# A T5 pair phase with its output projection a step later, a choice phase that fetches expert weights ahead of the row scatter, and weight loads moved to an earlier phase

## The reference, cut to what matters

```
for i in range(4):
    nx = t5_layer_norm(h, ln1[i])
    q, k, v = nx @ attn_q[i], nx @ attn_k[i], nx @ attn_v[i]      # 12 heads of 64
    attn = softmax(einsum('bqhd,bkhd->bhqk', q, k) + bias)         # 16 tokens each
    h = h + (attn @ v) @ attn_o[i]
    nx = t5_layer_norm(h, ln2[i])
    y = relu(nx @ ffn_wi[i]) @ ffn_wo[i]
    if i in (1, 3):
        y = y + moe_ffn(nx, gate_w[mi], moe_w1[mi], moe_w2[mi])    # top 2 of 8 experts, gelu
    h = h + y
return t5_layer_norm(h, ln_f)
```

## Time and profile before

| | before |
|---|---|
| runs | 1822.48, 1823.77, 1829.81 us; median 1823.77 |
| profiled execution | 1819.51 us, of which the profile's span is 1817.7 |
| PE busy | 1431.2 us (79%), mean granted clock 0.837 |
| DVE, ACT, POOL busy | 648.7, 467.2, 460.4 us |
| pair phase, first turn of the loop | from 303.35 us (first turn of unit 0) to 577.1 |
| choice phase, first turn | 578.36 to 632.2 us |
| pair and choice phase, second turn | from 765.64 and from 1035.79 us |

### The profile page before, as it was taken

How to read it: one execution, slowest core, us unless ns; L and a number is a source line. 1 busy time by engine, 2 the same in 40 slices (tenths; PEclk the granted TensorE clock), 3 DMA queues, 4 the chain that set the end, 5 groups by cost and what they waited for, 6 DMA issues and landing times. The chain is left out here.

```text
span 1817.7 us, 35567 instructions
## 1 busy us (share of the span) xinstructions
PE 1431.2 (79%) x14426; PEld 1136.1 (62%) x14426; DVE 648.7 (36%) x1668; ACT 467.2 (26%) x1226; POOL 460.4 (25%) x597
## 2 busy tenths in 40 slices
PE   5469743999987699589998769948735995876998
PEld 5255422788775489478877549934525995453766
DVE  3444652333232122233333222244551223463334
ACT  0420331333332011133333211113201332321121
POOL 0000461222221434222222143412324442230000
PEclk8778856999877899799998788979557998856999
DMA  4010006000000464400000047413015453010000
GB/s 119 0 27 12 5 1 228 2 2 2 2 2 2 166 214 125 122 18 2 2 3 2 1 160 234 133 53 111 3 75 184 146 173 116 8 55 4 27 27 17
DMA packets 57392, 117.44 MB, mean 65 GB/s; under 512 B 16656, under 2 KB 43540, under 8 KB 52400
## 3 DMA queue, kind: packets, MB, share of 16 engines
q1 hardware_dynamic: 40144, 60.38, 11.1%
q0 software_dynamic: 17088, 54.81, 8.6%
HBM read 140.33 MB, written 24.87 MB: 91 GB/s over the span
## 5 line engine op out<-in xcount | busy, mean ns | idle before, releaser
L1774 PE MATMUL bank<-t_wo,t_ctx 128*128 128x192 f32 x384 | 95.7, 416 | 29.0 <-ACT t_xa L1785 27.0
L1774 PEld LDWEIGHTS bank<-t_wo,t_ctx 128*128 128x128 f32 x384 | 86.6, 251 | 30.4 <-ACT t_ctx L1835 30.1
L1296 PE MATMUL bank<-xT,w 96*128 96x512 f32 x192 | 86.8, 611 | 15.5 <-ACTq L1350 15.5
L1149 PE MATMUL bank<-t_ew,t_hg 128*128 128x192 f32 x552 | 97.2, 327 | 0.0
L1389 DVE SCALAR_TENSOR_TENSOR h<-bank,cw,h 128x192 f32<-128x192 f32 x128 | 53.5, 418 | 100.3 <-PE bank L1312 83.8
L1149 PEld LDWEIGHTS bank<-t_ew,t_hg 128*128 128x128 f32 x552 | 88.7, 190 | 0.2
L329 PE MATMUL bank<-ident,rows 128*96 128x128 f32 x112 | 25.2, 418 | 77.1 <-DVE rows L312 77.1
L1181 ACT ACTIVATE t_hg<-bank 128x384 f32<-128x384 f32 x92 | 40.1, 488 | 173.2 <-PE bank L1137 140.3
L1177 ACT ACTIVATE l_hg<-bank,l_ew 128x128 f32<-128x128 f32 x186 | 51.4, 375 | 121.1 <-PE bank L1137 89.5
L1035 POOL DMA_INDIRECT t_ew<-in_t_moe,source x46 | 46.7, 1014 | 138.7 <-DVE t_og L1217 132.1
L1133 PE MATMUL bank<-t_xgT,t_ew 128*128 128x128 f32 x552 | 74.8, 289 | 4.2 <-DVE t_xgT L1208 3.3
(11 more groups left out here) (329 smaller groups left out, 3052.8 us busy)
## 6 DMA issues: line engine op xcount, KB each, us to landing
rows_in<-blank SPq DMA_DIRECT2D x2, 2967.0 KB
t_xg<-rows_in SPq DMA_DIRECT2D x46, 129.0 KB
wA<-in_t_wqkv SPq DMA_DIRECT2D x9, 576.0 KB
t_wo<-in_t_wo SPq DMA_DIRECT2D x9, 576.0 KB
t_qkv<-in_t_wqkv SPq DMA_DIRECT2D x9, 576.0 KB
w<-in_l_w SPq DMA_DIRECT2D x8, 576.0 KB, 5.3
rows_in<-blank SPq DMA_DIRECT2D x1, 3999.0 KB
l_xg<-rows_in SPq DMA_DIRECT2D x31, 129.0 KB
```

The source lines that it names most:

```text
L1149: mm = pe.matmul(k.bank[6 + b % 2][:, 0:DIM], k.hg[b % 2][:, m, :], w[:, SPLIT + m * DIM:SPLIT + (m + 1) * DIM], start=(m == 0), stop=(m = ...
L1296: mm = pe.matmul(k.bank[(u * FC + m) % 4][:], k.w1[s][:, c, m * P:(m + 1) * P], k.xT[:, c, n * HALF:(n + 1) * HALF], start=(c == 0), stop= ...
L1774: mm = pe.matmul(turn_bank[:, 0:DIM], buf.ctx[a % 2][:, m, :], layer(a).wo[:, m, :], start=(m == 0), stop=(m == FC - 1))
```

## The change

- Pair phase. On PE the output projection of w = s - 2 stands between queries and keys of step s (it was that of s - 1 at the step's end). The turn of n stands right after the keys, the turn of w after the values. ACT's list is reordered to match; its copy of the context stands ahead of the exponential for w >= 8 and at the end of the step else. DVE and POOL make the first norm's root and rows two units ahead instead of one.
- Choice phase. PE counts behind one pair of the hidden blocks instead of three. `plan_blocks` makes `source` first and `place_i` after it; POOL fetches the four weights, then scatters the rows.
- Loads. The tensors of a turn's first layer are allocated earlier, and their first contents are loaded in `quant_projection_phase` instead of the T5 norm phase. Those of the second layer (now in `wA`) are loaded in the pair phase, where PE waits for them at unit 8. `expert_blocks_phase` loads 8 tensors instead of 13.

```diff
     link(dve.tensor_reduce(first, square, AX_X, ALU.add))
-    dve.wait_ge(k.counted, 2)
...
-    dve.tensor_copy(k.place_i[:], k.place[:]).then_inc(k.chosen, 1)
     link(dve.tensor_tensor(end, first, used, ALU.add))
...
     dve.tensor_tensor(k.source[:, 0:nb], source, k.same[:, 0:nb], ALU.add).then_inc(k.chosen, 1)
+    dve.wait_ge(k.counted, 2)
...
+    dve.tensor_copy(k.place_i[:], k.place[:]).then_inc(k.chosen, 1)
...
@@ -1691,22 +1691,31 @@
                 return pe.transpose(turn_bank[:, P:2 * P], k.rows[:, u % NT, P:C_TOKEN], k.ident[:])
 
             for s in range(-1, units + 2):
-                u, a, w = s, s - 1, s - 2
+                u, a, w, n = s, s - 1, s - 2, s + 1
                 if 0 <= u < units:
                     qkv, x = layer(u).qkv, buf.xa[u % 2]
+                    if u == NT:
+                        pe.wait_ge(k.loaded, 16 * len(loads))
                     pe.wait_ge(k.first_kept, u + 1)
-                    if w >= 1 and w - 1 < NT:
-                        pe.wait_ge(k.relu_a, w)
-                        pe.wait_ge(k.relu_v, w)
                     features(pairs[0], qkv[:, 0, :], x).then_inc(k.q_made, 1)
-                    if u >= 2:
-                        pe.wait_ge(k.ctx_copied, u - 1)
+                if 0 <= w < units:
+                    pe.wait_ge(k.ctx_copied, w + 1)
+                    for m in range(FC):
+                        mm = pe.matmul(turn_bank[:, 0:DIM], buf.ctx[w % 2][:, m, :], layer(w).wo[:, m, :],
+                                       start=(m == 0), stop=(m == FC - 1))
+                    mm.then_inc(k.projected, 1)
+                if 0 <= u < units:
                     features(pairs[1], qkv[:, 1, :], x).then_inc(k.k_made, 1)
-                if 0 <= w < units:
-                    pe.wait_ge(k.normed_second, w + 1)
-                    pe.wait_ge(k.doubled_second, w + 1)
-                    turn(w).then_inc(k.turned_second, 1)
+                if n < units:
+                    pe.wait_ge(k.normed_first, n + 1)
+                    pe.wait_ge(k.doubled_first, n + 1)
+                    if w >= 0:
+                        pe.wait_ge(k.added, w + 1)
+                    turn(n).then_inc(k.turned_first, 1)
...
+                    if u == 1:
+                        pe.wait_ge(k.v_kept_a, 1)
+                        pe.wait_ge(k.v_kept_v, 1)
...
+                if 0 <= w < units:
+                    pe.wait_ge(k.normed_second, w + 1)
+                    pe.wait_ge(k.doubled_second, w + 1)
+                    if n < units:
+                        pe.wait_ge(k.first_kept, n + 1)
+                    turn(w).then_inc(k.turned_second, 1)
...
-                if 0 <= a < units:
-                    pe.wait_ge(k.ctx_copied, a + 1)
-                    pe.wait_ge(k.first_kept, min(s + 2, units))
...
+            def keep_context(a):
+                act.wait_ge(k.pv_done, a + 1)
+                if a >= 2:
+                    act.wait_ge(k.projected, a - 1)
...
+                if w >= NT and a < units:
+                    keep_context(a)
...
+                if w < NT and a >= 0:
+                    keep_context(a)
...
-            norm(0, 0, k.scaled_first, k.normed_first)
+            for u in range(2):
+                norm(u, 0, k.scaled_first, k.normed_first)
...
-                if s + 1 < units:
-                    norm(s + 1, 0, k.scaled_first, k.normed_first)
+                if s + 2 < units:
+                    norm(s + 2, 0, k.scaled_first, k.normed_first)
...
-            double(0, 0, k.squared_first, k.scaled_first, k.doubled_first)
-            pool.wait_ge(k.doubled_first, 1)
+            for u in range(2):
+                double(u, 0, k.squared_first, k.scaled_first, k.doubled_first)
+            pool.wait_ge(k.doubled_first, 2)
...
-                if s + 1 < units:
-                    double(s + 1, 0, k.squared_first, k.scaled_first, k.doubled_first)
+                if s + 2 < units:
+                    double(s + 2, 0, k.squared_first, k.scaled_first, k.doubled_first)
...
             pool.wait_ge(k.chosen, 2)
+            for i in range(W_SLOTS):
+                fetch_expert(pool, k, i, nb, weights)
+            pool.wait_ge(k.chosen, 3)
             send_rows(pool, k)
             pool.sem_inc(k.owner_known, 1)
-            pool.wait_ge(k.chosen, 3)
-            for i in range(W_SLOTS):
-                fetch_expert(pool, k, i, nb, weights)
...
-            first(0)
+            first(0, 0)
             pe.wait_ge(k.chosen, 1)
...
-            first(1)
-            pe.wait_ge(k.chosen, 2)
+            for i in range(2, 2 * FC, 2):
+                first(i // FC, i % FC)
+            pe.wait_ge(k.chosen, 3)
             second(0)
             second(1)
...
+        early = stage()
+        one = Kern()
+        one.qkv, one.wi = tensor(early, "t5_qkv", [P, 3, SPLIT]), tensor(early, "t5_wi", [P, SPLIT])
+        one.wo, one.wo2 = (tensor(early, f"t5_{name}0", [P, FC, DIM]) for name in ("wo", "wo2"))
+        one.ln1, one.ln2 = (tensor(early, f"t5_{name}0", [P, 2]) for name in ("ln1", "ln2"))
+
+        def pair_loads(first):
+
+            return ([(one.qkv[:, i, :], a["t5_wqkv"][first, :, i, :]) for i in range(3)]
+                    + [(one.wo[:], a["t5_wo"][first]), (one.wi[:], a["t5_wi"][first]), (one.wo2[:], a["t5_wo2"][first]),
+                       (one.ln1[:], a["t5_ln1"][first]), (one.ln2[:], a["t5_ln2s"][first])])
...
-            quant_projection_phase(k, k.wA[0:CH, 0:2 * 3 * DIM].rearrange("p (c n) -> p c n", c=2), qi, ki, qx, vx)
+            quant_projection_phase(k, k.wA[0:CH, 0:2 * 3 * DIM].rearrange("p (c n) -> p c n", c=2), qi, ki, qx, vx,
+                                   loads=pair_loads(0))
...
-            one.qkv = k.wA[:, 0:3 * SPLIT].rearrange("p (w n) -> p w n", w=3)
-            two.qkv = tensor(st, "t5_qkv", [P, 3, SPLIT])
...
-            norm_phase(k, k.h, 1e-5, loads=pair_loads(0) + [(bias16[:], a["t5_bias16"]), (k.bias[:], a["t5_lnf"])])
+            two = Kern()
+            two.qkv, two.wi, two.wo2 = k.wA[:, 0:3 * SPLIT].rearrange("p (w n) -> p w n", w=3), k.w1s[0][:, 0:SPLIT], k.w2[0]
+            two.wo, two.ln1, two.ln2 = tensor(st, "t5_wo1", [P, FC, DIM]), tensor(st, "t5_ln11", [P, 2]), k.ln2s
+
+            norm_phase(k, k.h, 1e-5, loads=[(bias16[:], a["t5_bias16"]), (k.bias[:], a["t5_lnf"])])
...
-                                  loads=[(two.wi, a["t5_wi"][2 * r + 1]), (two.wo2[:], a["t5_wo2"][2 * r + 1]),
+                                  loads=[(two.qkv[:], a["t5_wqkv"][2 * r + 1]), (two.wo[:], a["t5_wo"][2 * r + 1]),
+                                         (two.ln1[:], a["t5_ln1"][2 * r + 1]), (two.wi, a["t5_wi"][2 * r + 1]), (two.wo2[:], a["t5_wo2"][2 * r + 1]),
...
-    layers = (0, 1, 2, 3, 3, 3)
+    layers = (0, 1, 2, 3, 3)
```

More of the change, by code:

```diff
@@ L1028, in plan_blocks @@
     dve.tensor_tensor(k.source[:, 0:nb], source, k.same[:, 0:nb], ALU.add).then_inc(k.chosen, 1)
+    dve.wait_ge(k.counted, 2)
+    base = k.base[:, :, 0:n_e]
+    link(dve.scalar_tensor_tensor(base, first.unsqueeze(1).broadcast_to([P, NT, n_e]), float(P),
+                                  rank_bank[:, 0:NT * n_e].rearrange("p (t e) -> p t e", e=n_e), ALU.mult, ALU.add))
+    for c in range(2):
+        link(dve.tensor_tensor(k.picked[:, c, :, 0:n_e], k.sel[:, c, :, 0:n_e], base, ALU.mult))
+        link(dve.tensor_reduce(k.place[:, c, :], k.picked[:, c, :, 0:n_e], AX_X, ALU.add))
+    link(dve.tensor_tensor(k.picked[:, 0, :, 0:n_e], k.sel[:, 1, :, 0:n_e],
+                           k.iota[:, 0:n_e].unsqueeze(1).broadcast_to([P, NT, n_e]), ALU.mult))
+    link(dve.tensor_reduce(k.rows[:, :, C_SECOND], k.picked[:, 0, :, 0:n_e], AX_X, ALU.add))
+    dve.tensor_copy(k.place_i[:], k.place[:]).then_inc(k.chosen, 1)
 def fetch_expert(pool, k, i, nb, weights):
@@ L1791, in _ @@
             keep_turned(buf.xa[0], layer(0).ln1).then_inc(k.first_kept, 1)
+            def keep_context(a):
+                act.wait_ge(k.pv_done, a + 1)
+                if a >= 2:
+                    act.wait_ge(k.projected, a - 1)
+                banks = pairs[1] + pairs[2]
+                for j in range(QUADS):
+                    ins = act.activation(buf.ctx[a % 2][:, :, j * QUAD:(j + 1) * QUAD],
+                                         banks[j][:, 0:FC * QUAD].rearrange("p (m q) -> p m q", q=QUAD), ACT.Copy)
+                ins.then_inc(k.ctx_copied, 1)
             for s in range(units + 2):
@@ L1800, in _ @@
                     ins.then_inc(k.q_kept, 1)
+                if 0 <= w < units:
+                    act.wait_ge(k.added, w + 1)
+                    square(w, 1).then_inc(k.squared_second, 1)
+                if u < units:
                     act.wait_ge(k.k_made, u + 1)
@@ L1818, in _ @@
                     act.activation(buf.v[u % 2][:, 0:FF // 2], pairs[2][0][:, 0:FF // 2], ACT.Copy).then_inc(k.v_kept_a, 1)
+                if 0 <= w < units:
+                    act.wait_ge(k.turned_second, w + 1)
```

(11 more changed lines are left out.)

107 lines of the change are left out of this document (25 added, 82 removed).

## The result

| | runs | median |
|---|---|---|
| before | 1821.43, 1822.48, 1823.77, 1829.81 us | 1823.12 |
| after | 1732.31, 1735.08, 1737.48, 1737.93 us | 1736.28 |

The ratio is 0.951, with a 95% interval of 0.949 to 0.953: 87 us less. The profiled execution of after took 1732.31 us, its span is 1730.4 and its mean granted clock 0.860.

What follows compares the result with a forecast made beforehand. PE was taken to bound the T5 pair phase, never idle in plain steps but waiting 2.31 us in gate steps. Gains 54.1 + 11.0 + 18.4 = 83.5 us; 1823.8 - 83.5 = 1740 us, range 1725 to 1762.

Steps and rivals of the forecast that it cites:

- Plain steps: Pair phase, plain steps: PE's work stays 15.70 us and a new wait of 0.3 makes the step 16.0 us.
- new wait of 0.3: Plain step, PE before wi, waiting for the second norm's turned rows copied by ACT: 0.3 us, bounds 0 and 0.63.
- Gate steps: Pair phase, gate steps: 11.8 us of PE work plus a 0.6 us wait before PV, 12.4 us instead of 17.1.
- Ends: Pair phase, first queries to projection 14: 223.8 us against 253.3 and 248.4 before, gains 29.5 + 24.6 = 54.1 us.
- Loads: T5 norm phase without its 13 loads: bias phase starts 11.0 us earlier, bounds 9.6 and 12.3; block phase gains nothing.
- Choice phase: Choice phase with early counts and fetches before scatters: 9.2 us less per loop turn, 18.4 in all, bounds 4 and 13.
- The queue: Choice phase, POOL's queue: scattered rows stand behind the weights, early scatters land late, the last does not; sum unchanged.
- Rival 3: Choice phase: POOL cannot write scatter descriptors while weights are on their way; gain 4 per turn, time 1751; chance 0.07.
- rival 2: Pair phase: the new waits are not there, time 1728, or 1721 with `second` not drawn out either; chance 0.10.

Runs made afterwards that it cites:

- late_values: The changed kernel with three 128x768 memsets on DVE ahead of its copy of the values in steps 11 to 15; median 1764.45 us.
- before_again: The kernel before, unchanged, run once more for its profile beside the second group of variants; 1820.46 us (one run).
- after_again: The changed kernel, unchanged, run once more beside its variants in the second group; median 1728.51 us.
- both_first: The changed kernel with DVE's values copy ahead of its norm and, in plain steps, ACT's turned rows for w ahead of its values copy; median 1719.92 us.

## Why the prediction was right, point by point

- **Plain steps.** 16.0 predicted, 15.89 measured, but not for my reason. ACT's `keep_turned` stands where I laid it, and its copy of the values starts 2.35 us behind PE's values as in the earlier trace rows, but the two overlap and the rows are ready at 353.45, as PE comes at 353.50. The 0.19 above before's 15.70 is in PE's own segments: projection 347.51 - 345.46 = 2.05 (1.95 before), `wo2` 359.06 - 357.00 = 2.06 (1.96), the turn ahead of the scores 0.1 longer, the keys 0.1 shorter, the rest even. So the step of the prediction that failed is the new wait of 0.3; its bound of 0 was the right end, and the 0.19 that stood in its place was in no term, so that 16.0 fits by luck.
- **Gate steps.** 12.4 predicted; 12.59 measured with the wait, 12.5 on the average of a loop turn's. The wait before PV is 0.36 and not 0.6 and is missing in the last two, the gate 0.64 and not 0.5, turns and projection a little longer. That the wait of 2.31 took the clock with it, and that a short one would not, carried most of the term. Before has one gate step with the same wait at the full clock, from PV (L1740) to PV in the second loop turn:

```profile
930.30 1.16 PE L1740 MATMUL bank<-t_ptb,t_v 32*64 32x32 f32 x96
...
944.64 1.08 PE L1740 MATMUL bank<-t_ptb,t_v 32*64 32x32 f32 x86
```

It took 14.35 us; the steps with the same wait and a projection of 4.18 us took 17.0 to 17.1. So of the 4.5 us that a step lost, about 2.75 are clock and 1.75 the shorter wait and what else changed. late_values confirms that a wait put in brings the clock down, with costs of 1.5 to 3.1 us.
- **Ends.** 223.8 us from the first queries to projection 14 predicted (6 x 12.4 is 74.4 and not 74.6, so 223.6), 222.85 measured. Behind it I had left everything as before; at the full clock projection 14 itself took 2.22 instead of 4.21, and from its start to the choice phase 1.3 us were gained. Pair phases in all: 54.1 predicted, 31.8 + 27.3 = 59.1 in the first profiles, 28.8 + 25.8 = 54.6 between before_again and after_again. One after_again phase contains a stretch at a lower clock, behind 0.94 us in which PE issued nothing.
- **Loads.** 11.0 predicted, 17.10 - 6.05 = 11.05 measured from DVE's scaled rows to the bias phase; every profile with the loads moved has 6.0 to 6.1 there, every one without 16.7 to 17.2. That the quantised projection phase hides them holds (26.57 us before, 26.44 after). That fewer loads give the block phases nothing holds too: they were 2.7 and 1.6 us shorter in the first profiles, but between before_again and after_again 2.2 longer and 1.3 shorter.
- **Choice phase.** The mis-sized term: 9.2 per loop turn predicted; 7.2 and 7.5 with the hole, 11.8 and 12.4 without. Two steps failed. The fetches start 10.1 us behind the start of the phase and not 8.4: counts at 5.2 instead of 4.4, since the first hidden blocks run at a granted clock of 0.56 (0.67 before), and 4.9 from counts to fetch instead of 4.1, of which 0.97 stand between DVE's last operation and POOL's first issue (0.31 ahead of the first scatter before). And I let `second` be drawn out for good. Without the hole it ends 36 to 37 us behind the start, the x rows end last, and the next phase starts at 41.2 to 42.3, near the other bound I gave, 13.
- **The queue.** Rival 3 is out: 20 indirect transfers in a row, the scatters 1.28 to 1.33 us apart and the fetches 1.3 to 1.6, with no stop, so the stop that I derived from the Trainium skill ("DMA: Bandwidth & Descriptors", section "SWDGE vs HWDGE vs iDMA") does not occur at this depth. Its other rule, in the section "Two DMAs through the same engine are not ordered" (within one queue of an engine, descriptors start in order), agrees with the trace: in the first loop turn of after_again the scatters' packets (4128 bytes) start at 562.9, though the first scatter was issued at 554.0, and by then all but 10 of the weights' 512 (9216 bytes) have started. Its early scatters land 9.8 us behind their issue, its last 2.5, before_again's all about 2.5. As worked out in the prediction, that costs nothing, since the last scatter comes when the weights are through.

Scatters of after_again (553 to 556 and 570 to 576 us) and before_again (592 to 596): issues, median us to landing.

```profile
rows_in<-rows,place_i POOLq DMA_INDIRECT x2, 9.8
```

```profile
rows_in<-rows,place_i POOLq DMA_INDIRECT x4, 2.5
```

```profile
rows_in<-rows,place_i POOLq DMA_INDIRECT x3, 2.5
```

The total, 1740, was within 4 us of the first median, 1736.28, and part of that is luck: the pair phases gained 5 us more than their term, the block phases 4.3 that no term had, and the choice phases 3.7 less, held back by the hole. Where the hole is absent the forecast is 10 to 12 us too high (1728.51, 1729.89): inside the range of 1725 to 1762, but below the forecast's own 1731 to 1752 and at the 1728 that rival 2 gave for both waits missing.

## What to carry to other kernels

When PE waits a few us for a turned or copied tile in every step, it can pay to move the consumer a step later instead of speeding the producer: here the wait of 2.31 us took 2.75 us of clock with it in most steps. An order written out by hand is worth a layout of every engine's list against PE's, since the place of the wait that comes next is then known: of the two waits laid out here one was 0.36 us and not 0.6, the other did not come. Where one engine issues all indirect transfers, putting those with the long landing first was worth 6.7 us per phase here; splitting them left a long one to end alone and cost 2.7 to 2.9.

## What the runs showed of the hardware that I had not expected

- A hole in the instructions of two engines at once: in the first profile of after, PE issued five matmuls in 6.7 us and DVE left finished banks for 10.95 us, and PE came back 2 us behind the end of the last scatter (570.91 against 568.96); before's first profile has one too. The same programs did not show it in their later profiles. The cause is open.
- A small one is in every profile but late_values': within PV of the second gate step of each loop turn PE issues nothing for 0.3 to 1.2 us, whatever the kernel (before 0.41, after 0.29, after_again 0.94, both_first 1.07 in the first turn).
- A wait of 3.0 us on PE was followed by 3.8 us at a granted clock of 0.59 in one loop turn and by 4.7 us at 0.50 in the other. In before, a wait of 2.31 us was followed by a projection of 4.18 us in seven steps and of 2.19 in one, so the same wait does not always cost the clock.
- The same twelve matmuls of 128x192 take 2.05 us from start to the next group's start where the group ahead of them uses 64 or 32 of PE's rows (queries or PV, in after), and 1.95 where it uses 128 (turns or `wo2`, in before). The keys show the same: 2.41 us behind the queries' last group in before, 2.30 behind the projection in after.
